# Two fused adaLN/FFN layers on one core: gates by block transposes on VectorE, T1's sums on VectorE, other places for W5's copies and C12's results

## The chip, the cores and the metric

One core of one Trainium2 chip runs the whole program. The metric is the time of one execution in microseconds (us), median of several runs. TensorE (PE in the profile) multiplies, VectorE (DVE), ScalarE (ACT) and GpSimd (POOL) do the elementwise work, SyncE (SP) issues most DMAs.

## The reference, cut to what matters

```python
def layer(x):                              # twice: layer 0, layer 1; x is 8 x 256 tokens of 1024
    c = x @ W0.T + b0 + lora(x, adapter of the batch)            # "cond", rank 16
    probs = softmax(c @ W_router.T)                              # 8 experts
    top2 of probs, renormalized -> w_dense[token, expert], 0 for the other six
    h = einsum('td,erd->ter', c, lora_A)                         # 8 experts x rank 16 = 128 rows
    f = c @ W1.T + b1 + 2.0 * einsum('ter,eor,te->to', h, lora_B, w_dense)
    return x + f
```

## The kernel before

`fused_layers` first multiplies the two dense weights of a layer (the fold: `fold`, lines 489 to 491, E = [W1, lora_A, router], 1160 columns, against W0), then runs the folded product over 2048 tokens. Numbers are fp32, kept as a high and a low part in fp32r; a product of two such numbers takes three matmuls (hi*hi, hi*lo, lo*hi). Whatever is split has its cast on ScalarE (high part) and a subtraction on VectorE (low part, helper `sub`, L977).

Tokens come in chunks of 512; two chunks are a **pair** g (0 and 1 in layer 0, 2 and 3 in layer 1), and a pair's product is done by Strassen-Winograd: seven products W1, W2, W6, W5, W3, W7, W4 of half size, each of four output tiles m of 12 matmuls (L605), on the input blocks B11, B21 (chunk 0), B12, B22 (chunk 1) and the sums T3 = B22 - B12, T2 = T3 + B11, T1 = B22 - T2, T4 = B21 - T2. GpSimd makes the four sums. The results C11, C12, C21, C22 gather in PSUM banks; `keep_w1`, `keep_w5` (ScalarE) and `keep_u2`, `keep_w57` (VectorE) carry partial results out of banks, `out_c11` to `out_c22` (VectorE, L1186) add bias and residual. `low_and_experts` (L621 and three matmuls) adds the adapter and expert parts to a bank.

Each engine runs a fixed list in the order of the code, and semaphores join the lists. For each chunk tb of a pair:

- `routers` (16 matmuls L564, then 24 into H_BANK) yields the low-rank, router and expert rows; `adapters` and `low_rest` on VectorE make `low_mv` of them; `inner_low` (L587) adds the low-rank part to the 128 rows h.
- The logits: four matmuls of 128 x 8 (L609), one to a group of 128 tokens, between the matmuls of a W product. Tokens are then on partitions.
- `routing` (VectorE): bias, `max`, `max_index`, comparison with an iota, softmax of two (`gap`, the exponential on ScalarE in `top_exp`), and `gates`: tokens on partitions, 128 columns.
- Four fp32 transposes on TensorE (L614) turn the gates into H_BANK, in front of which h was copied out by ScalarE (`inner`, h_sb). `gated` multiplies both (hg), ScalarE and VectorE split hg (`hg_split`), and `low_and_experts` needs it.

In chunk 1 TensorE's order is: routers, W6 m0, `inner_low`, W6 m1 to m3, W5 m0 and m1, W3 m0 with `low_and_experts`, W3 m1 with `low_and_experts`, W5 m2 and m3, W3 m2, m3, W7, W4. W3 m adds into the bank of W5 m, so it waits for W5 m's copy (w5_done). W5 needs both parts of T1.

SyncE's list holds the loads of the weight tiles: a ring of seven buffers (`load_ring`, n = 0 to 27 for the 28 tiles of a pair; tile n may load once tile n - 7 is used), between them the stores and the loads of the next pair's blocks. In a pair that has a successor in its layer (pairs 0 and 2), the load of B21 (1 MB) stands ahead of ring loads 23, 24, 25 and waits for r21_done, that is for GpSimd's `add_12`, `make_t4` and `add_21`, twelve additions in a row that begin at the first `keep_u2`. Ring load 23 brings the tile of W7 m3.

## Time and profile before

| | us |
|---|---|
| median of 3 runs (lowest, highest) | 686.79 (685.77, 687.58) |
| the profiled execution: its own time | 686.49 |
| its span, first to last instruction | 684.8 |
| busy in the span: PE, DVE, ACT, POOL | 678.8, 423.3, 231.6, 261.6 |
| chain that ended last: PE's share | 97% |

The page's second part shows PE busy at 9 tenths or more in all slices but the first and the last, and a granted TensorE clock of 9 tenths or more in all. In the timelines below a row is a start in us, a time taken, an engine, a line, an operation and its tiles; "xN" means N instructions in a row merged, and a bracket names idle time ahead of it and who ended it.

### The profile page before, as it was taken

What the parts mean: (1) busy time and instruction counts of PE and PEld (TensorE: products, weight loads), DVE (VectorE), ACT (ScalarE), POOL (GpSimd) and SP (SyncE); (2) the same over time, 40 slices, a digit from 0 to 9 for tenths busy, and PEclk for the clock granted to TensorE, in tenths of its full rate; (3) what the DMA queues carried; (4) which work ended last, traced back from release to release, by engine and by line L of the source; (5) the groups of instructions that cost most, each with busy time, mean ns of one, the idle gap of its engine ahead of it and who ended that gap; (6) DMA issues with size and microseconds to landing.
All of it is one profiled execution on the core that took longest, in us unless ns stands there. A gap on an engine that the chain in (4) does not pass through costs nothing.

```text
span 684.8 us, 9215 instructions
## 1 busy us (share of the span) xinstructions
PE 678.8 (99%) x3299; PEld 598.0 (87%) x3299; DVE 423.3 (62%) x719; ACT 231.6 (34%) x429; POOL 261.6 (38%) x217
## 2 busy tenths in 40 slices
PE   8999999999999999999999999999999999999997
PEld 7999999888888888888899999998888888888886
DVE  5664667868855474862673753788698437738423
ACT  6444244645221034220514344266352302422200
POOL 2373023036583150395134433030647625105930
PEclk9999999999999999999999999999999999999999
DMA  8345756993768944547742755689846886535633
GB/s 291 115 156 185 262 196 205 392 386 130 245 194 327 326 123 124 157 145 254 276 176 72 235 167 182 246 279 371 333 127 212 282 342 196 181 116 168 199 106 123
DMA packets 74132, 147.25 MB, mean 215 GB/s; under 512 B 6948, under 2 KB 38308, under 8 KB 73958
## 3 DMA queue, kind: packets, MB, share of 16 engines
q1 hardware_dynamic: 70678, 138.20, 58.7%
q10 hardware_dynamic: 1872, 6.36, 2.9%
q0 software_dynamic: 1536, 2.10, 1.1%
q8 instruction: 26, 0.43, 0.3%
q14 instruction: 20, 0.16, 0.1%
HBM read 98.42 MB, written 47.33 MB: 213 GB/s over the span
## 4 chain that ended last, share of the span: by engine, by line
PE 97%; DMA 1%; SPq 1%; ACT 0%; DVE 0%; issue 0%
PE ps L605 45%; PE ps L489 15%; PE ps L490 15%; PE ps L491 15%; PE ps L564 4%; PE ps L621 2%; DMA e_raw<-in_ext 1%; PE ps L614 1%; SPq L289 0%; PE ps L587 0%; ACT e_hl L715 0%; SPq L266 0%; DVE w_hl L977 0%; DVE w L1186 0%; ACT w_hl L724 0%
## 5 line engine op out<-in xcount | busy, mean ns | idle before, releaser
L605 PE MATMUL ps<-x_hl,a_hl 128*128 128x512 f32 x1344 | 317.8, 394 | 0.0
L605 PEld LDWEIGHTS ps<-x_hl,a_hl 128*128 128x128 f32 x1344 | 251.3, 188 | 53.3 <-issue 0.3
L489 PE MATMUL ps<-e_hl,w_hl 128*128 128x384 f32 (+1 forms) x432 | 146.2, 338 | 0.8 <-DVE e_hl L977 0.7
L490 PE MATMUL ps<-e_hl,w_hl 128*128 128x384 f32 (+1 forms) x432 | 145.8, 337 | 0.0
L491 PE MATMUL ps<-e_hl,w_hl 128*128 128x384 f32 (+1 forms) x432 | 145.5, 337 | 0.0
L489 PEld LDWEIGHTS ps<-e_hl,w_hl 128*128 128x128 f32 x432 | 81.3, 188 | 2.7 <-issue 1.3
L490 PEld LDWEIGHTS ps<-e_hl,w_hl 128*128 128x128 f32 x432 | 81.3, 188 | 0.0
L491 PEld LDWEIGHTS ps<-e_hl,w_hl 128*128 128x128 f32 x432 | 81.3, 188 | 0.0
L977 DVE TENSOR_TENSOR x_hl<-x_raw,x_hl 128x512 fp32r<-128x512 f32 x64 | 60.8, 1004 | 8.4 <-ACT x_hl L811 8.4
L1363 POOL TENSOR_TENSOR w<-x_raw 128x512 f32<-128x512 f32 x16 | 23.8, 1515 | 103.8 <-DMA x_raw<-in_xT 32.7
L977 DVE TENSOR_TENSOR w_hl<-w_raw,w_hl 128x1024 fp32r<-128x1024 f32 (+2 forms) x24 | 20.6, 868 | 58.0 <-ACT w_hl L702 51.1
L1345 POOL TENSOR_TENSOR f_sum<-p_raw 128x512 f32<-128x512 f32 x8 | 12.5, 1558 | 111.7 <-ACT p_raw L760 111.7
L1382 POOL TENSOR_TENSOR x_sum<-x_raw,c 128x512 f32<-128x512 f32 x16 | 24.2, 1542 | 69.3 <-PE ps L491 69.3
L977 DVE TENSOR_TENSOR x_hl<-x_sum,x_hl 128x512 fp32r<-128x512 f32 x32 | 39.6, 1251 | 15.3 <-ACT x_hl L835 9.8
L1038 DVE SCALAR_TENSOR_TENSOR acc<-e_hl,b_sb,acc 128x1160 f32<-128x1160 f32 x32 | 45.6, 1424 | 0.8
L760 ACT COPY p_raw<-ps 128x384 f32<-128x384 f32 (+1 forms) x48 | 22.3, 480 | 70.0 <-PE ps L491 69.9
L811 ACT CAST x_hl<-x_raw 128x512 fp32r<-128x512 f32 x64 | 35.7, 618 | 26.2 <-PE ps L605 12.9
L1186 DVE SCALAR_TENSOR_TENSOR x_raw<-ps,bias_sb,x_raw 128x512 f32<-128x512 f32 x32 | 22.8, 741 | 32.5 <-PE ps L491 32.3
L1416 POOL TENSOR_TENSOR w<-w,x_raw 128x512 f32<-128x512 f32 x16 | 22.0, 1375 | 36.8 <-DVE w L980 36.8
L1394 POOL TENSOR_TENSOR x_raw<-x_raw,u 128x512 f32<-128x512 f32 x16 | 22.0, 1404 | 29.9 <-DVE u L980 29.9
L564 PE MATMUL ps<-x_hl,s_hl 128*128 128x512 f32 x128 | 31.3, 395 | 0.0
L977 DVE TENSOR_TENSOR px_hl<-p_raw,px_hl 128x128 fp32r<-128x128 f32 x16 | 11.5, 717 | 30.7 <-ACT pr_hl L764 30.7
(118 smaller groups left out, 896.9 us busy)
## 6 DMA issues: line engine op xcount, KB each, us to landing
a_hl<-form_scratch SPq DMA_DIRECT2D x112, 512.0 KB, 5.0
form_scratch<-f_hl SPq DMA_DIRECT2D x56, 512.0 KB, 7.3
...
```

Of the source, the lines that this page charges most:

```text
L489: nc.tensor.matmul(dst, w_hi, m_hi, start=start, stop=False, skip_group_check=again)
L490: nc.tensor.matmul(dst, w_hi, m_lo, start=False, stop=False, skip_group_check=again)
L491: return nc.tensor.matmul(dst, w_lo, m_hi, start=False, stop=stop, skip_group_check=again)
L564: last = nc.tensor.matmul(ps[:, S_BANK, :], s_hl[:, k, :], x_hl[:, slots[block], k % KH, hl, :], start=(k + hl == 0), stop=(k + hl == KT))
L605: last = nc.tensor.matmul(ps[:, bank, :], a_hl[:, n % NM, k, w, :], x_hl[:, slot, k, x, :], start=start and i == 0, stop=i == 3 * KH - 1, ...
L760: ins = nc.scalar.copy(p_raw[:, pair % 2, half, o:o + n], ps[:, fold_bank(r, ob), 0:n])
L811: nc.scalar.copy(x_hl[:, slot, k, 0, :], raw_of(block, k)).then_inc(x_hi[block], 1)
L977: return nc.vector.tensor_tensor(dst, a, b, ALU.subtract)
L1038: ins = nc.vector.scalar_tensor_tensor(acc[:], e_hl[:, k, hl, 0:EXT].bitcast(f32), b0_sb[:, k:k + 1], acc[:], op0=ALU.mult, op1=ALU.add)
L1186: return nc.vector.scalar_tensor_tensor(dst, ps[:, bank, :], bias_sb[:, k:k + 1], rest_of_sum, op0=ALU.add, op1=ALU.add)
L1363: nc.gpsimd.tensor_tensor(w57[:, k, :], raw_of(B22, k), raw_of(B12, k), ALU.subtract).then_inc(S["t3_done"], 1)
L1382: nc.gpsimd.tensor_tensor(x_sum[:, SLOT_OF[g % SUPER][T1], k, 1, :], raw_of(B22, k), c21[:, k, :], ALU.subtract).then_inc(S["t1_done"], 1)
```

## The change

- **Logits.** One matmul of 128 x 512 in `inner_low` takes the place of the four 128 x 8. Its weights `rt_cols` are the eight router columns, copied sixteen times side by side by ScalarE (`router_cols`, one copy of 128x128 for each chunk). Each expert's logit of each token is so on 16 partitions, tokens along the columns.
- **Gates.** `routing` turns the logits by VectorE's transpose of 32 x 32 blocks, so that 16 groups of 32 tokens stand on the partitions; it finds the best two experts by reductions and comparisons (the first of equals by a rank), makes for each 32 partitions the gates of two experts, 16 columns each, and turns them back by blocks into hg. The four transposes on TensorE, the identity matrix and `inner`'s copy are gone. `gated` now multiplies H_BANK with hg, and its low half is a function of its own, `gated_low`.
- **T1.** VectorE makes T1's four sums (`make_t1`, after `low_rest` of chunk 1), not GpSimd. T1's and T3's splits both stand ahead of `routing(g, 1)`.
- **Order.** In chunk 1 TensorE does W3 m0 and W3 m1 one after the other, and then both `low_and_experts`. ScalarE copies W5's m1, m2, m3 ahead of T4's casts. VectorE does `gated`, u2's m0, `gated_low`, u2's other three, then C12's m0 and m1 ahead of T4's splits.

```diff
                 else:
                     pe.wait_ge(S["stack_in"], l + 1)
                 pe.wait_ge(S["eye_done"], 2)
+                pe.wait_ge(S["rt_done"], u + 1)
+                nc.tensor.matmul(ps[:, S_BANK, :], rt_cols[:], low_mv[tb][:], start=True,
+                                 stop=True).then_inc(S["pe_logit"], 1)
                 nc.tensor.matmul(ps[:, H_BANK, :], stack[tb][:, D:D + ER], low_mv[tb][:], start=False,
                                  stop=True).then_inc(S["pe_h"], 1)
 
-            def product(g, j, m, bank, start, logits_of=None, gates_of=None):
+            def product(g, j, m, bank, start):
 
 
...
-
-                    pe.wait_ge(S["h_done"], 2 * g + gates_of + 1)
-                    pe.wait_ge(S["gate_done"], 2 * g + gates_of + 1)
                 for i in range(3 * KH):
                     k, (w, x) = i // 3, ((0, 0), (0, 1), (1, 0))[i % 3]
                     last = nc.tensor.matmul(ps[:, bank, :], a_hl[:, n % NM, k, w, :], x_hl[:, slot, k, x, :],
                                             start=start and i == 0, stop=i == 3 * KH - 1, skip_group_check=not start)
-                    if logits_of is not None and i < TT:
-                        tb = logits_of
-                        logit = nc.tensor.matmul(ps[:, S_BANK, i * NE:(i + 1) * NE], low_mv[tb][:, i * P:(i + 1) * P],
-                                                 stack[tb][:, D + ER:EXT], start=True, stop=True)
-                        if i == TT - 1:
-                            logit.then_inc(S["pe_logit"], 1)
-                    if gates_of is not None and i < TT:
-                        gate = nc.tensor.transpose(ps[:, H_BANK, i * P:(i + 1) * P], gates[:, i, :], ident_sb[:])
-                        if i == TT - 1:
-                            gate.then_inc(S["pe_gate"], 1)
                 last.then_inc(S["pe_m"], 1)
 
             def low_and_experts(half, tb, m, bank, start=False):
...
                                 pe.wait_ge(S["u2_done"], KH * g + m - 1)
-                            product(g, W5, m, BANK_C12[m], True, gates_of=None if m else 1)
+                            product(g, W5, m, BANK_C12[m], True)
                         for m in (m2, m2 + 1):
                             pe.wait_ge(S["w5_done"], KH * g + m + 1)
                             product(g, W3, m, BANK_C12[m], False)
-                            if m == 0:
-                                pe.wait_ge(S["hg_lo"], 2 * g + 2)
-                            low_and_experts(0, 1, m, BANK_C12[m])
+                            if m >= 2:
+                                low_and_experts(0, 1, m, BANK_C12[m])
+                        if m2 == 0:
+                            pe.wait_ge(S["hg_lo"], 2 * g + 2)
+                            for m in range(2):
+                                low_and_experts(0, 1, m, BANK_C12[m])
...
 
+            def router_cols(l, g, tb):
+
...
+                               stack[tb][:, D + ER:EXT].bitcast(f32).unsqueeze(1).broadcast_to([P, P // NE, NE])
+                               ).then_inc(S["rt_done"], 1)
+
             def first_stack(l):
...
                     adapters(l, g, 1, more)
-                    t1_split(g, range(2))
-                    inner(g, 1)
-                    t1_split(g, range(2, 3))
+                    router_cols(l, g, 1)
+                    t1_split(g)
                     top_exp(g, 1)
-                    t1_split(g, range(3, 4))
                     keep_w5(g, 0)
                     hg_split(g, 1)
-                    keep_w5(g, 1)
+                    for m in range(1, KH):
+                        keep_w5(g, m)
                     t4_split(g)
-                    for m in range(2, KH):
-                        keep_w5(g, m)
...
+            def make_t1(g):
+
+                dve.wait_ge(S["pe_hx"], 2 * g + 2)
+                for k in range(KH):
+                    dve.wait_ge(S["t2_done"], KH * g + k + 1)
+                    sub(x_sum[:, SLOT_OF[g % SUPER][T1], k, 1, :], raw_of(B22, k), c21[:, k, :]
+                        ).then_inc(S["t1_done"], 1)
+
...
+                ins = nc.vector.transpose(by_token[:].rearrange("p g c -> p (g c)"), ps[:, S_BANK, :])
+                ins.then_inc(S["logit_read"], 1)
+                dve.wait_ge(S["logit_read"], u + 1)
+                chain(nc.vector.tensor_tensor(lg, lg,
+                                              bias_r[:].unsqueeze(1).broadcast_to([P, GR, NE]), ALU.add))
+                for i, (v, m, gate) in enumerate(((lg, ma, ga), (lg2, mb, gb))):
+                    chain(nc.vector.tensor_reduce(top[i][:], v, AXIS.X, ALU.max))
+                    chain(nc.vector.tensor_tensor(m[:], v, over(top[i], NE), ALU.is_equal))
+                    if i:
+                        sub(gap[:], top[1][:], top[0][:]).then_inc(S["gap_done"], 1)
+                    chain(nc.vector.tensor_tensor(m[:], m[:], ranks, ALU.mult))
+                    chain(nc.vector.tensor_reduce(first_of[i][:], m[:], AXIS.X, ALU.max))
+                    if i == 0:
+                        chain(nc.vector.tensor_tensor(m[:], over(first_of[i], NE), ranks, ALU.is_equal))
+                        chain(nc.vector.scalar_tensor_tensor(lg2, m[:], -3.0e38, lg, op0=ALU.mult, op1=ALU.add), False)
+                    chain(nc.vector.tensor_tensor(gate[:], over(first_of[i], WANT), wanted, ALU.is_equal))
                 dve.wait_ge(S["exp_done"], u + 1)
                 chain(nc.vector.tensor_scalar(den[:], ex[:], 1.0, None, ALU.add))
                 chain(nc.vector.reciprocal(wb[:], den[:]))
                 chain(nc.vector.tensor_scalar(wa[:], wb[:], 2.0, None, ALU.mult))
-                chain(nc.vector.tensor_tensor(den[:], ex[:], wa[:], ALU.mult))
-                chain(nc.vector.tensor_tensor(ma[:], ma[:], wa[:].broadcast_to([P, TT, NE]), ALU.mult), False)
-                chain(nc.vector.tensor_tensor(mb[:], mb[:], den[:].broadcast_to([P, TT, NE]), ALU.mult))
-                nc.vector.tensor_tensor(gates[:].rearrange("p t (e r) -> p (t e) r", r=R),
-                                        *(m[:].rearrange("p t e -> p (t e)").unsqueeze(2)
-                                          .broadcast_to([P, TT * NE, R]) for m in (ma, mb)),
-                                        ALU.add).then_inc(S["gate_done"], 1)
+                chain(nc.vector.tensor_tensor(den[:], ex[:], wa[:], ALU.mult), False)
+                chain(nc.vector.tensor_tensor(ga[:], ga[:], over(wa, WANT), ALU.mult))
+                chain(nc.vector.tensor_tensor(gb[:], gb[:], over(den, WANT), ALU.mult))
+                chain(nc.vector.tensor_tensor(by_token[:].rearrange("p g (n r) -> p g n r", r=R),
+                                              *(m[:].unsqueeze(3).broadcast_to([P, GR, WANT, R]) for m in (ga, gb)),
+                                              ALU.add))
+                chain(nc.vector.transpose(hg[:], by_token[:].rearrange("p g c -> p (g c)")))
 
             def gated(g, tb):
                 u = 2 * g + tb
-                dve.wait_ge(S["h_done"], u + 1)
-                dve.wait_ge(S["pe_gate"], u + 1)
-                nc.vector.scalar_tensor_tensor(hg[:], h_sb[:], bias_sb[:, KT:KT + 1], ps[:, H_BANK, :],
+                dve.wait_ge(S["pe_h"], u + 1)
+                nc.vector.scalar_tensor_tensor(hg[:], ps[:, H_BANK, :], bias_sb[:, KT:KT + 1], hg[:],
                                                op0=ALU.add, op1=ALU.mult).then_inc(S["hg_done"], 1)
-                dve.wait_ge(S["hg_hi"], u + 1)
+
+            def gated_low(g, tb):
+                dve.wait_ge(S["hg_hi"], 2 * g + tb + 1)
                 sub(hg_hl[:, tb, 1, :], hg[:], hg_hl[:, tb, 0, :].bitcast(f32)).then_inc(S["hg_lo"], 1)
 
...
                     low_rest(g, 1)
+                    make_t1(g)
                     out_c11(g, 2)
                     out_c11(g, 3)
-                    made_split(g, T1, range(2))
+                    made_split(g, T1)
+                    sum_split(g, T3, w57)
                     routing(g, 1)
-                    made_split(g, T1, range(2, 4))
-                    sum_split(g, T3, w57)
-                    for m in range(KH):
+                    gated(g, 1)
+                    keep_u2(g, 0)
+                    gated_low(g, 1)
+                    for m in range(1, KH):
                         keep_u2(g, m)
-                    gated(g, 1)
                     if more:
                         s_split(l, 2 * s + 2)
+                    out_c12(g, 0)
+                    out_c12(g, 1)
                     made_split(g, T4)
-                    for m in range(KH):
-                        out_c12(g, m)
+                    out_c12(g, 2)
+                    out_c12(g, 3)
                     if more:
...
                 for s in range(SUPER):
                     g = SUPER * l + s
-                    for k in range(KH):
-                        make_t1(g, k)
                     for m in range(KH):
                         add_12(g, m)
                     for k in range(KH):
```

TensorE, pair 0, chunk 1, from the last tile ahead of `inner_low` (low_mv_86 and stack_68 are chunk 1's buffers), before:

```order
L605 MATMUL ps<-x_hl,a_hl 128x512 x12
L587 MATMUL ps<-low_mv_86,stack_68 128x512
L605 MATMUL ps<-x_hl,a_hl 128x512
L609 MATMUL ps<-stack_68,low_mv_86 128x8
L605 MATMUL ps<-x_hl,a_hl 128x512
L609 MATMUL ps<-stack_68,low_mv_86 128x8
L605 MATMUL ps<-x_hl,a_hl 128x512
L609 MATMUL ps<-stack_68,low_mv_86 128x8
L605 MATMUL ps<-x_hl,a_hl 128x512
L609 MATMUL ps<-stack_68,low_mv_86 128x8
```

and after:

```order
L607 MATMUL ps<-x_hl,a_hl 128x512 x12
L591 MATMUL ps<-low_mv_86,rt_cols 128x512
L593 MATMUL ps<-low_mv_86,stack_68 128x512
L607 MATMUL ps<-x_hl,a_hl 128x512 x84
L613 MATMUL ps<-low_mv_86,stack_68 128x512
```

The eight small matmuls are gone from between the W matmuls, one of full width has come in front of the one that was there, and 84 W matmuls now stand together.

VectorE, pair 0, chunk 1, from C11's first two results to the start of `routing`, before:

```order
L1186 SCALAR_TENSOR_TENSOR x_raw<-ps,bias_sb,x_raw 128x512 x2
L1138 SCALAR_TENSOR_TENSOR low_mv_86<-sx_r,sign_sb,ps 32x512
L977 TENSOR_TENSOR low_mv_86<-sx,low_mv_86 32x512
L1186 SCALAR_TENSOR_TENSOR x_raw<-ps,bias_sb,x_raw 128x512 x2
L977 TENSOR_TENSOR x_hl<-x_sum,x_hl 128x512 x2
L1148 TENSOR_TENSOR lg<-ps,bias_r 128x32
```

and after:

```order
L1207 SCALAR_TENSOR_TENSOR x_raw<-ps,bias_sb,x_raw 128x512 x2
L1151 SCALAR_TENSOR_TENSOR low_mv_86<-sx_r,sign_sb,ps 32x512
L982 TENSOR_TENSOR low_mv_86<-sx,low_mv_86 32x512
L982 TENSOR_TENSOR x_sum<-x_raw,c_62 128x512 x4
L1207 SCALAR_TENSOR_TENSOR x_raw<-ps,bias_sb,x_raw 128x512 x2
L982 TENSOR_TENSOR x_hl<-x_sum,x_hl 128x512 x4
L982 TENSOR_TENSOR x_hl<-w_61,x_hl 128x512 x4
L1167 STREAM_TRANSPOSE by_token<-ps 128x512
```

T1's sums (x_sum) came in, and T1's last two and T3's four splits (x_hl from x_sum and from w_61) moved from behind `routing` to ahead of it.

ScalarE, pair 0, chunk 1, from T1's casts to T4's casts (w_61 is W5's copy, hg_hl the high part of hg), before:

```order
L817 CAST x_hl<-x_sum 128x512 x2
L867 COPY h_sb<-ps 128x512
L817 CAST x_hl<-x_sum 128x512
L871 ACTIVATE ex<-gap 128x4
L817 CAST x_hl<-x_sum 128x512
L893 COPY w_61<-ps 128x512
L877 CAST hg_hl<-hg 128x512
L893 COPY w_61<-ps 128x512
L835 CAST x_hl<-x_sum 128x512 x4
L893 COPY w_61<-ps 128x512 x2
```

and after:

```order
L860 CAST rt_cols<-stack_68 128x128
L811 CAST x_hl<-x_sum 128x512 x4
L879 ACTIVATE ex<-gap 128x16
L901 COPY w_61<-ps 128x512
L885 CAST hg_hl<-hg 128x512
L901 COPY w_61<-ps 128x512 x3
L829 CAST x_hl<-x_sum 128x512 x4
```

`inner`'s copy h_sb went, the router columns' copy came, and W5's m2 and m3 moved ahead of T4's four casts (x_sum). W5's m1 stands behind the cast of hg as before.

## Rows read from the trace of the kernel before

**Rows 1.** The page's first part: busy us (share of span) and instructions.
```profile
PE 678.8 (99%) x3299; PEld 598.0 (87%) x3299; DVE 423.3 (62%) x719; ACT 231.6 (34%) x429; POOL 261.6 (38%) x217
```

**Rows 2.** Waits of TensorE: who waited for whom, us, times, longest.
```profile
PE ps L489 <- DVE e_hl L977: 0.7, 2, 0.4
```

**Rows 3.** Groups of instructions, TensorE: busy us, mean ns, idle before.
```profile
L614 PE MATMUL ps<-ident_sb,gates 128*128 128x128 f32 x32 | 8.7, 272 | 0.0
L609 PE MATMUL ps<-stack,low_mv 128*128 128x8 f32 x32 | 5.4, 168 | 0.0
```

**Rows 4.** TensorE's timeline, chunk 1 of pair 0: start us, us taken, instruction.
```profile
166.60 2.88 PE L605 MATMUL ps<-x_hl,a_hl 128*128 128x512 f32 x12
...
169.54 0.39 PE L605 MATMUL ps<-x_hl,a_hl 128*128 128x512 f32 x1
...
186.84 0.39 PE L621 MATMUL ps<-low_mv,stack 128*128 128x512 f32 x1
...
204.07 21.92 PE L605 MATMUL ps<-x_hl,a_hl 128*128 128x512 f32 x96
```

**Rows 5.** VectorE's timeline in the same stretch.
```profile
162.91 0.87 DVE L1122 TENSOR_SCALAR low_b<-ps,mul_sb 32x256 f32<-32x256 f32 x2
...
166.03 0.76 DVE L1138 SCALAR_TENSOR_TENSOR low_mv<-sx_r,sign_sb,ps 32x512 fp32r<-32x512 f32 x1
...
167.54 1.41 DVE L1186 SCALAR_TENSOR_TENSOR x_raw<-ps,bias_sb,x_raw 128x512 f32<-128x512 f32 x2
...
177.30 2.49 DVE L977 TENSOR_TENSOR x_hl<-w,x_hl 128x512 fp32r<-128x512 f32 x4
179.70 2.48 DVE L980 TENSOR_TENSOR u<-ps,u 128x512 f32<-128x512 f32 x4
182.10 0.74 DVE L1179 SCALAR_TENSOR_TENSOR hg<-h_sb,bias_sb,ps 128x512 f32<-128x512 f32 x1
```

**Rows 6.** Groups, VectorE, whole run: operations like the new ones.
```profile
L1102 DVE STREAM_TRANSPOSE acc_t<-acc 128x1152 f32<-128x1152 f32 x2 | 2.7, 1356 | 0.0
...
L1107 DVE TENSOR_REDUCE part_sb<-acc_t 128x36 f32<-128x1152 f32 x2 | 2.7, 1345 | 0.0
...
L1159 DVE TENSOR_TENSOR ma<-iota_sb,top_f 128x32 f32<-128x32 f32 x8 | 1.5, 193 | 0.3
```

**Rows 7.** ScalarE's timeline, same stretch.
```profile
182.87 0.62 ACT L877 CAST hg_hl<-hg 128x512 fp32r<-128x512 f32 x1 [0.69 <-DVE hg L1179]
```

**Rows 8.** GpSimd's timeline, same stretch.
```profile
166.91 6.40 POOL L1382 TENSOR_TENSOR x_sum<-x_raw,c 128x512 f32<-128x512 f32 x4 [5.40 <-PE ps L491]
180.47 5.49 POOL L1394 TENSOR_TENSOR x_raw<-x_raw,u 128x512 f32<-128x512 f32 x4 [7.16 <-DVE u L980]
...
192.00 5.95 POOL L1403 TENSOR_TENSOR c<-x_raw,u 128x512 f32<-128x512 f32 x4
```

**Rows 9.** SyncE's queue, same stretch: start of issue, us.
```profile
197.98 0.38 SPq L360 DMA_DIRECT2D x_raw<-in_xT  x1
198.46 1.84 SPq L373 DMA_DIRECT2D a_hl<-form_scratch  x3
```

**Rows 10.** Ring load 23 of pair 0, issued at 198.46.
```profile
DMA to landing us min/median/max: 8.5/8.5/8.5
```

**Rows 11.** The same load of pair 2, issued at 535.71.
```profile
DMA to landing us min/median/max: 9.1/9.1/9.1
```

**Rows 12.** GpSimd's timeline, chunk 1 of pair 1: T1's sums.
```profile
278.09 4.23 POOL L1382 TENSOR_TENSOR x_sum<-x_raw,c 128x512 f32<-128x512 f32 x3 [29.12 <-PE ps L491]
```

**Rows 13.** TensorE's timeline there: W6 begins.
```profile
277.78 2.88 PE L605 MATMUL ps<-x_hl,a_hl 128*128 128x512 f32 x12
```

**Rows 14.** TensorE's timeline, chunk 0 of pair 0.
```profile
136.41 0.39 PE L587 MATMUL ps<-low_mv,stack 128*128 128x512 f32 x1
```

**Rows 15.** ScalarE's timeline, chunk 0 of pair 0.
```profile
136.84 0.58 ACT L867 COPY h_sb<-ps 128x512 f32<-128x512 f32 x1 [1.64 <-PE ps L587]
...
139.08 1.07 ACT L888 COPY u<-ps 128x512 f32<-128x512 f32 x2
```

109 lines of the change are left out of this document (54 added, 55 removed).

## The prediction

> **What bounds the kernel now.** The first view to read is the page's busy line: TensorE is busy 678.8 of 684.8 us [rows 1]. That alone could hide pauses, since the ends of matmuls are modelled, so the second view is the list of TensorE's waits: behind the start-up only 0.7 us in two pieces, both in the fold, and none in the token stage [rows 2]. Every matmul there starts as soon as the one ahead lets it, so the kernel is a queue of TensorE work, and two questions decide the change: what the removed and added matmuls cost in that queue, and whether any wait that was early before is now late. Durations don't answer the first. The groups give 272 ns for a transpose and 168 ns for a logit matmul [rows 3], but neighbours overlap. The timeline does: 96 W matmuls in a row take 21.92 us; less the last one's own 0.39 that is 21.53 us between 96 starts, 0.2266 us each. Between 169.54 and 186.84 there are 72 of them (W6 m1 to m3, W5 m0 and m1, W3 m0), four logit matmuls and four transposes [rows 4]. 72 x 0.2266 = 16.32 of the 17.30 us; so eight small ones cost 0.98 us, 0.12 each.
>
> **TensorE's sum.** There are eight chunks. Removed: 8 x 0.98 = 7.8 us. Added: eight matmuls of 128 x 512, 8 x 0.2266 = 1.8 us. Net 6.0 us less, all of it on the path. The low bound is that a chunk's eight cost no more than 0.9 (some of the 0.98 could be the hand-over at `inner_low`): 5.4 less. A higher bound than 6.0 has no row. The Trainium skill (TensorE: Matmul & The Clock Gate, Part 4: PE-mode transpose) gives about 275 ns for a transpose in a kernel's context; the duration in this trace agrees, 272. Taken as cost in the queue it would make the 32 transposes alone worth 8.8 us, against 32 x 0.12 = 3.9 by the timeline, and the time would come out about 5 us lower than below. I take the timeline.
>
> **New lateness, chunk 1 of pair 0.** Both chunks' savings move TensorE ahead: 0.75 us (0.98 - 0.23) by the start of chunk 1's W6, 1.50 by its W3. VectorE doesn't move with it, since its chain starts at 162.91 behind T2's splits, which hang on loads and GpSimd [rows 5]. So I walk that chain. Up to 167.54 nothing changes. Then T1's sums: four subtractions of 128x512 at the spacing of T3's splits, which ran with GpSimd idle (177.30 to 179.70, 0.60 each), 2.40, to 169.94. C11's pair 1.42, to 171.36. T1's four splits 2.40, T3's 2.40, to 176.16. GpSimd has nothing until u2, so none of these is slowed.
>
> The new `routing` isn't in the trace; its price comes from like operations [rows 6]. A line through 193 ns for 32 elements and 1356 ns for 1152 has 1.04 ns per element; a reduction of 1152 costs the same (1345). That makes 0.69 us for 512 elements, 0.29 for 128, 0.19 for 32 and 0.17 for 16. Nearly every one waits for the one ahead, which I put at 0.04 (VectorE's hg ends at 182.84 and ScalarE starts on it at 182.87 [rows 5, 7]). Two transposes and the last addition, 3 x 0.73 = 2.2; eleven of 128 elements, 11 x 0.33 = 3.6; four of 32, 0.9; five of 16, 1.0; less 0.2 where there is no wait: 7.5 us. Between 6.8 (all handovers free) and 9 (0.06 more on each of 24) is possible.
>
> So `gated` starts at 183.66 and hg is ready at 184.40 (0.74 [rows 5]). **W5's m1** is copied by ScalarE only behind hg's cast: 184.43 + 0.62 [rows 7] + 0.54 = 185.6. W3 m1 wants it at 186.84 + 0.91 (the four matmuls of `low_and_experts`), less 0.91 since these now stand behind W3 m1 as well, less 1.50: 185.34. **0.3 us late**, in a place where nothing was late before. hg's low half itself is ready by 186.4 at the latest, wanted at 188.1.
>
> **Ring load 23.** `keep_u2` m0 comes behind `gated`: 183.66 + 0.66 + 0.69 = 185.0, where it used to release GpSimd by 180.47. GpSimd's twelve additions took 180.47 to 197.95 [rows 8], 17.5 us; with fewer of VectorE's two-input operations beside them perhaps 16.5. r21_done comes at 201.5 to 202.5. The 1 MB load of B21 left at 197.98, with r21_done, and ring load 23 0.48 us behind it [rows 9], landing 8.5 us later [rows 10]. It now lands at 210.5 to 211.5. W7 m3 wants it at 204.07 + 3 x 2.72 - 1.50 = 210.73 [rows 4]. The wait was covered by 5 us before and is now at its edge: pair 0 loses 0.3 to 0.8 in all (the two delays are one behind the other, not added). Pair 2 is built alike, but there the same load takes 9.1 us [rows 11]: 0.4 to 1.5. Pairs 1 and 3 have no such load. There, T1's sums can start 0.31 us behind W6's first matmul (GpSimd did, at 278.09 against 277.78 [rows 12, 13]), in pair 0 1.69 behind (167.54 against 166.60 - 0.75), so their chain has 1.4 us more and W5's copy comes 1.1 early. Both pairs together: 0.7 to 2.3 us lost, I take 1.5, in the middle, since the unknowns lie on both sides.
>
> **Chunk 0.** In pairs 0 and 2 ScalarE's exponential stands ahead of `keep_w1` m0, which W2 m0 wants. The matmul's result is seen 0.43 us after its start (136.41 to 136.84 [rows 14, 15]); gap is ready 4.0 us into routing by the same prices; exponential and copy 0.14 + 0.6 [rows 15]: 5.2 after `inner_low` starts. W2 m0 comes after two matmuls and two tiles, 26 x 0.2266 = 5.9. Covered by 0.7. In pairs 1 and 3 m0 is copied earlier and three tiles lie between. **At nothing** stand: GpSimd's four T1 sums (6.4 us [rows 8], GpSimd isn't waited for there), the copy of the router columns (some 0.3 us of ScalarE, 1.5 us ahead of need behind the adapters' copies), `inner`'s copy, C12's new place (its stores leave earlier), the smaller constants.
>
> **The sum.** 684.8 - 6.0 + 1.5 = 680.3 of span; the execution's own time is 1.7 above its span, 682.0, and the median 0.3 above that execution (686.79 against 686.49): **682.3 us**.
>
> **Rivals.**
> 1. Nothing comes late: routing at 6.8 or GpSimd's twelve at under 16.5. 686.8 - 6.0 = 680.8. For it: both delays are tenths on chains of 20 to 40 us. Against: two places would have to be covered in two pairs.
> 2. The reload takes the gain: stores, B21 and rings 23 to 27 are now issued closer together, and ring 23 lands 10 to 11 us after issue. Pairs 0 and 2 then lose some 2.5 each: 686.8 - 6.0 + 5.0 = 685.8. For it: 9.1 us in pair 2 already. Against: ring load 22 and C12's first stores are out of the way by then.
> 3. Slower: `routing` on VectorE sets the end. If it takes x us more than 7.5, pairs 0 and 2 lose x each in chunk 1, and beyond 1.1 the other pairs', beyond 0.7 chunk 0 of pairs 0 and 2: 2x + 2(x - 1.1) + 2(x - 0.7). That and the 1.5 above eat the 6.0 at x = 1.35, a routing of 8.9 us; at x = 2, 691. Place: ScalarE's `hg_split` and `top_exp`, with W5's and W1's copies queued behind. Against: the lines above fit three kinds of operation. The Trainium skill (VectorE: DVE Perf Modes, Rules for kernel authors) sends 128x128 transposes to TensorE where PSUM will do, and asks for few operations in a chain on VectorE; both speak for this rival. No row here shows a chain of 128-element operations.
> 4. The matmul of 128 x 512 doesn't take the normal slot, or the small ones were free: the sum is 2 to 3 less, about 685. Rows 4 speak against it.
>
> **Chances.** Forecast 0.55; rival 1 0.17; rival 2 0.14; rival 3 0.08; rival 4 0.06. The range of 8 in 10 goes from rival 1 to near rival 2: 680.7 to 685.5. A measurement tells about 0.3%, 2.1 us, from no change. Faster by more (below 684.7): 0.55 + 0.17 + parts of 2 and 4, 0.80. Within: 0.13. Slower: 0.07.
>
> **What would show it.** In the changed kernel's trace: TensorE with 56 matmuls fewer (64 gone, 8 come), W matmuls still 0.2266 apart; `routing` from transpose to `gated` 7.5 us; a pause of TensorE ahead of W3 m1 on ScalarE's copy w and one ahead of W7 m3 on a DMA of a_hl, in pairs 0 and 2 only; T1's sums at 0.6 us each. Wrong would be: pauses in chunk 0, routing above 8.5 us, or any pause in pairs 1 and 3.

## The result, and the profile after

| | before | changed |
|---|---|---|
| median, us | 686.50 (685.77 to 687.58, 6 runs) | 681.44 (680.25 to 681.99, 6 runs) |
| profiled execution, us | 686.49 | 681.37 |
| its span, us | 684.8 | 679.7 |

The ratio is 0.9922, 95% interval 0.9912 to 0.9933: the changed kernel is 5.1 us, 0.8%, faster. The forecast was 682.3 (680.7 to 685.5).

The page's first part, to be read beside [rows 1] (busy us, share of the span, instructions):

```profile
PE 673.0 (99%) x3243; PEld 592.9 (87%) x3243; DVE 467.6 (69%) x724; ACT 226.6 (33%) x429; POOL 238.7 (35%) x201
```

TensorE has 56 instructions less and 5.8 us less of busy time. VectorE has 44 us more, 69% instead of 62%, and that in itself cost nothing. What it did cost stands in TensorE's waits (who waited for whom, us in all, times, longest), beside [rows 2]:

```profile
PE ps L621 <- DVE hg_hl L1239: 1.6, 1, 1.6
PE ps L607 <- ACT w L901: 0.6, 2, 0.4
PE ps L492 <- DVE e_hl L982: 0.6, 2, 0.4
PE ps L607 <- DMA a_hl<-form_scratch: 0.2, 1, 0.2
```

The first is the start-up and the third the fold, both as before. The second and the fourth are new: the token stage, which had no pause, has three. In TensorE's timeline (start, us taken, instruction, idle before it and who ended that) they are:

```profile
150.42 2.97 PE L607 MATMUL ps<-x_hl,a_hl 128*128 128x512 f32 x12 [0.21 <-DMA a_hl<-form_scratch]
...
169.77 15.80 PE L607 MATMUL ps<-x_hl,a_hl 128*128 128x512 f32 x69
185.98 3.04 PE L607 MATMUL ps<-x_hl,a_hl 128*128 128x512 f32 x12 [0.41 <-ACT w L901]
...
203.36 11.95 PE L607 MATMUL ps<-x_hl,a_hl 128*128 128x512 f32 x52
...
519.79 3.02 PE L607 MATMUL ps<-x_hl,a_hl 128*128 128x512 f32 x12 [0.20 <-ACT w L901]
```

The first line is W2 m3 in chunk 0 of pair 0, the lines at 185.98 and 519.79 are W3 m1 in chunk 1 of pairs 0 and 2. A pause costs 0.16 us more than the idle time in brackets, since a matmul's 0.39 is counted to its end while the next may start 0.2266 after its start. So the three cost 0.37, 0.57 and 0.36: 1.3 us. The matmuls right behind a pause are a little slower too (3.04 us for twelve instead of 2.88), 0.4 us in all. No row after 203.36 shows a wait for ring load 23. Pairs 1 and 3 have no pause at all.

VectorE's timeline, chunk 1 of pair 0, is the chain that the prediction walked; lines between the first and the second transpose are routing's small operations:

```profile
167.93 2.50 DVE L982 TENSOR_TENSOR x_sum<-x_raw,c 128x512 f32<-128x512 f32 x4
170.46 1.41 DVE L1207 SCALAR_TENSOR_TENSOR x_raw<-ps,bias_sb,x_raw 128x512 f32<-128x512 f32 x2
171.79 2.49 DVE L982 TENSOR_TENSOR x_hl<-x_sum,x_hl 128x512 fp32r<-128x512 f32 x4
174.19 2.49 DVE L982 TENSOR_TENSOR x_hl<-w,x_hl 128x512 fp32r<-128x512 f32 x4
176.59 0.71 DVE L1167 STREAM_TRANSPOSE by_token<-ps 128x512 f32<-128x512 f32 x1
...
183.29 0.71 DVE L1193 STREAM_TRANSPOSE hg<-by_token 128x512 f32<-128x512 f32 x1
184.04 0.75 DVE L1198 SCALAR_TENSOR_TENSOR hg<-ps,bias_sb,hg 128x512 f32<-128x512 f32 x1
...
185.48 1.81 DVE L982 TENSOR_TENSOR hg_hl<-hg,hg_hl 128x512 fp32r<-128x512 f32 x1
```

Routing takes 184.04 - 176.59 = 7.45 us. ScalarE's timeline there shows W5 m1's copy behind hg's cast:

```profile
184.82 0.62 ACT L885 CAST hg_hl<-hg 128x512 fp32r<-128x512 f32 x1 [3.42 <-DVE hg L1198]
185.35 0.58 ACT L901 COPY w<-ps 128x512 f32<-128x512 f32 x1
```

The chain that ended last was TensorE's for 97% of the span before and is for 75% now. From the pause ahead of W3 m1 it goes back through this copy and VectorE's chain to GpSimd's T2, and from there to the 1 MB load of B22 (start, us until it landed):

```profile
134.85 14.19 DMA x_raw<-in_xT
```

So the pause on ScalarE's copy also begins with a DMA. This load let GpSimd start at 149.16, where it started at 148.78 before, and VectorE's chain began 0.4 us later with it (163.31 for 162.91).

### The profile page after: what moved, and what is told of

Same layout as the page of the kernel before. It is cut to its first block, busy times and chain, and to the rows that moved or that the text cites. A ratio compares the mean times of both kernels' runs of the same rounds, so it can differ in the third digit from the quotient of the medians.

```text
span 679.7 us, 9094 instructions
## 1 busy us (share of the span) xinstructions
PE 673.0 (99%) x3243; PEld 592.9 (87%) x3243; DVE 467.6 (69%) x724; ACT 226.6 (33%) x429; POOL 238.7 (35%) x201
## 4 chain that ended last, share of the span: by engine, by line
PE 75%; DMA 9%; DVE 8%; POOL 3%; SPq 2%; issue 2%; ACT 1%; POOLq 0%; ACTq 0%
PE ps L607 33%; PE ps L492 13%; PE ps L493 12%; PE ps L494 12%; DMA form_scratch<-f_hl 4%; PE ps L567 2%; DMA x_raw<-in_xT 2%; DMA x_raw<-x_scratch 2%; PE ps L613 2%; POOL w L1393 2%; DVE x_hl L982 2%; POOL c L1405 1%; DVE f_hl L982 1%; DMA e_raw<-in_ext 1%; DVE x_raw L1207 1%
## 5 line engine op out<-in xcount | busy, mean ns | idle before, releaser
L607 PE MATMUL ps<-x_hl,a_hl 128*128 128x512 f32 x1344 | 310.1, 390 | 0.8 <-ACT w L901 0.6
L982 DVE TENSOR_TENSOR x_hl<-x_raw,x_hl 128x512 fp32r<-128x512 f32 x64 | 70.5, 1154 | 3.9 <-ACT x_hl L805 3.8
L1393 POOL TENSOR_TENSOR w<-x_raw 128x512 f32<-128x512 f32 x16 | 25.6, 1633 | 107.3 <-DMA x_raw<-in_xT 33.3
L1375 POOL TENSOR_TENSOR f_sum<-p_raw 128x512 f32<-128x512 f32 x8 | 12.5, 1566 | 111.3 <-ACT p_raw L755 111.3
L982 DVE TENSOR_TENSOR x_hl<-x_sum,x_hl 128x512 fp32r<-128x512 f32 x32 | 35.5, 1169 | 23.3 <-ACT x_hl L829 23.3
L1207 DVE SCALAR_TENSOR_TENSOR c<-ps,bias_sb,c 128x512 f32<-128x512 f32 x16 | 11.7, 749 | 26.2 <-PE ps L494 26.2
L567 PEld LDWEIGHTS ps<-x_hl,s_hl 128*128 128x128 f32 x128 | 23.8, 188 | 5.6 <-DVE x_hl L982 0.9
```

The lines of the kernel that those rows point to most:

```text
L567: last = nc.tensor.matmul(ps[:, S_BANK, :], s_hl[:, k, :], x_hl[:, slots[block], k % KH, hl, :], start=(k + hl == 0), stop=(k + hl == KT))
L607: last = nc.tensor.matmul(ps[:, bank, :], a_hl[:, n % NM, k, w, :], x_hl[:, slot, k, x, :], start=start and i == 0, stop=i == 3 * KH - 1, ...
L982: return nc.vector.tensor_tensor(dst, a, b, ALU.subtract)
L1393: nc.gpsimd.tensor_tensor(w57[:, k, :], raw_of(B22, k), raw_of(B12, k), ALU.subtract).then_inc(S["t3_done"], 1)
```

## The experiments

A plain median stands beside the span of the one profiled execution, and a ratio is always to executions of the kernel before that were timed together with that run (medians 686.23 to 686.51). Expectations were written before each run.

### Parts of the change alone

**w5_ahead**: is the pause ahead of W3 m1 the place of W5 m1's copy behind hg's cast?

```diff
                     keep_w5(g, 0)
+                    keep_w5(g, 1)
                     hg_split(g, 1)
-                    for m in range(1, KH):
+                    for m in range(2, KH):
                         keep_w5(g, m)
```

> The changed kernel with one edit: in chunk 1 ScalarE copies W5's m1 ahead of hg's cast instead of behind it. Theory (TensorE's queue less 6.0 us, and what is missing to that is two late copies): the two pauses ahead of W3 m1 (W3 m1 started 0.57 us late in pair 0 and 0.37 in pair 2 by the changed kernel's trace) are gone, span 679.7 - 0.9 = 678.8, time about 680.5. Rival (these pauses are paid somewhere else anyway, by hg's cast, which now comes later, or by ring load 23): the span stays at 679.5 to 679.9 and a new pause of the same size stands ahead of low_and_experts or of W7 m3.

Measured: 681.01 (679.55 to 682.25), ratio 0.9923 (0.9909 to 0.9936), span 680.5. Both pauses on the copy are gone, as said, and still the span of the profiled execution, the slowest of five, is no shorter, because the other kind has grown. TensorE's waits, and its timeline in chunk 0 of pair 0:

```profile
PE ps L607 <- DMA a_hl<-form_scratch: 1.2, 2, 0.8
PE ps L492 <- DVE e_hl L983: 1.2, 1, 1.2
...
148.42 2.99 PE L607 MATMUL ps<-x_hl,a_hl 128*128 128x512 f32 x12 [0.47 <-DMA a_hl<-form_scratch]
152.16 3.00 PE L607 MATMUL ps<-x_hl,a_hl 128*128 128x512 f32 x12 [0.75 <-DMA a_hl<-form_scratch]
```

W2 m2 and W2 m3 wait there for ring loads 6 and 7 (1.5 us with the 0.16 of each), and the fold lost 0.6 more than in the changed kernel's execution. Over all executions the ratio is the changed kernel's, 0.9923 against 0.9922. So the 0.9 us of the edit are seen in the waits, not in the times; and there is a second cause, of which the prediction knew nothing, that varies from one execution to the next.

**t1_alone**: the kernel before, with T1's sums on VectorE only.

```diff
+                    make_t1(g)
                     out_c11(g, 2)
...
-                    for k in range(KH):
-                        make_t1(g, k)
                     for m in range(KH):
                         add_12(g, m)
```

> The kernel before with one part of the change: VectorE makes T1's four sums, GpSimd does not; nothing else. Theory (the gain is TensorE's queue alone): nothing late, TensorE has the same matmuls, 686.5 within 0.5 us. Rival (part of the gain comes from the port that VectorE and GpSimd share, or from the order of the elementwise work): 1 to 3 us faster, 683.5 to 685.5. T1's sums should take 0.6 us each on VectorE, T1's last split be ready near 177.8 us of pair 0, wanted at 178.2.

Measured: 685.93 (685.83 to 686.66), ratio 0.9999 (0.9989 to 1.0008), span 684.2. GpSimd is relieved and nobody waited for it: nothing gained.

**t1_gpsimd**: the changed kernel with T1's sums back on GpSimd (the same edit, turned round).

> The changed kernel with T1's sums back on GpSimd, all else as changed. GpSimd's four take some 5.6 to 6.4 us from W6's first matmul on, so T1's last split ends near 174.2 us of pair 0 and routing starts near 176.6, the same as with VectorE's sums. Theory: the move of T1 is worth between nothing and 0.6 us in a pair, the time is 681.4 to 683. Rival (the move is what keeps the longer chain on VectorE in time): pauses of 1 to 2 us in each pair ahead of W3 m1, 685 to 689.

Measured: 680.73 (680.62 to 682.52), ratio 0.9922 (0.9907 to 0.9937), span 680.8. No difference can be measured. In the trace VectorE reaches routing at 176.02 instead of 176.59, the copy comes 0.6 earlier, and the pause ahead of W3 m1 is gone. That isn't the edit's doing: VectorE's chain began 0.67 earlier in this execution (162.64 for 163.31), and from there to routing it took 13.4 us against 13.3. VectorE is rid of 2.5 us of sums, but what runs beside GpSimd's sums is slower, T1's splits (4.50 us instead of 2.49) and `low_rest`'s subtraction (1.29 instead of 0.68):

```profile
162.64 0.87 DVE L1135 TENSOR_SCALAR low_b<-ps,mul_sb 32x256 f32<-32x256 f32 x2
...
166.00 5.94 POOL L1411 TENSOR_TENSOR x_sum<-x_raw,c 128x512 f32<-128x512 f32 x4 [4.77 <-PE ps L494]
...
166.55 1.29 DVE L982 TENSOR_TENSOR low_mv<-sx,low_mv 32x512 fp32r<-32x512 f32 x1
...
169.19 4.50 DVE L982 TENSOR_TENSOR x_hl<-x_sum,x_hl 128x512 fp32r<-128x512 f32 x4
```

So the place of T1's sums is worth nothing, as was expected. This execution, the slowest of four, lost 1.6 us on ring loads 6 and 7 again, in pair 2.

**w3_order_before**: the changed kernel with TensorE's old order, `low_and_experts` m0 between W3 m0 and W3 m1.

```diff
+                            if m == 0:
+                                pe.wait_ge(S["hg_lo"], 2 * g + 2)
+                            low_and_experts(0, 1, m, BANK_C12[m])
-                            if m >= 2:
-                                low_and_experts(0, 1, m, BANK_C12[m])
-                        if m2 == 0:
-                            pe.wait_ge(S["hg_lo"], 2 * g + 2)
-                            for m in range(2):
-                                low_and_experts(0, 1, m, BANK_C12[m])
```

> The changed kernel with TensorE's old order in chunk 1: W3 m0, its low_and_experts, W3 m1, its low_and_experts. The low half of hg is then wanted 2.7 us earlier, at 185.4 in pair 0, and was ready at 187.3 in the changed kernel. Theory: a wait on hg_hl of 1.9 us in pairs 0 and 2 takes the place of the 0.57 and 0.37, and 0.1 in pairs 1 and 3; together some 2.9 more, 684.3 us. Rival (the low half's 1.81 us are an effect of GpSimd beside it and the order hides nothing that counts): 681.4 to 682.5.

Measured: 684.39 (684.21 to 685.14), ratio 0.9974 (0.9965 to 0.9984), span 683.2. As expected: hg's low half is late by 1.5 and 1.7 us in pairs 0 and 2.

```profile
186.94 0.50 PE L613 MATMUL ps<-low_mv,stack 128*128 128x512 f32 x1 [1.53 <-DVE hg_hl L979]
```

**c12_behind_t4** and **w5_behind_t4**: the two moves of VectorE's and ScalarE's order, undone one at a time.

```diff
-                    out_c12(g, 0)
-                    out_c12(g, 1)
                     made_split(g, T4)
-                    out_c12(g, 2)
-                    out_c12(g, 3)
+                    for m in range(KH):
+                        out_c12(g, m)
```

> Edit: the changed kernel, with C12's first two results again behind T4's splits on VectorE (the kernel before had all four there); their stores leave SP's queue ahead of ring loads 22 and 23. In the changed kernel T4's splits end at 203.8 in pair 0, so C12 m0's store would leave at about 204.7 and ring load 22 right behind it at 205 (191.2 now); it lands 4.5 to 5.8 later, 209.5 to 210.7, and W7 m2 wants it at 208.8. Ring load 23, behind a store and B21's 1 MB, lands at 213 to 214, wanted 211.5 plus what is already lost. Expected 2 lost in each of pairs 0 and 2, 1 in each of pairs 1 and 3: +6, 687.4 (684 to 690), pauses on a_hl ahead of W7 m2 and m3. Rival (C12's place was worth nothing, as the prediction has it under the edits at nothing): 681.4 to 682.

Measured: 691.29 (688.66 to 692.36), ratio 1.0067 (1.0045 to 1.0088), span 688.8: more than expected. The pauses are where they were said to be (TensorE, pair 0):

```profile
209.44 3.00 PE L607 MATMUL ps<-x_hl,a_hl 128*128 128x512 f32 x12 [0.75 <-DMA a_hl<-form_scratch]
214.50 13.87 PE L607 MATMUL ps<-x_hl,a_hl 128*128 128x512 f32 x60 [2.06 <-DMA a_hl<-form_scratch]
```

and each pair pays 0.9 (pair 3) to 3.1, 8.5 in all.

```diff
                     keep_w5(g, 0)
                     hg_split(g, 1)
-                    for m in range(1, KH):
-                        keep_w5(g, m)
+                    keep_w5(g, 1)
                     t4_split(g)
+                    for m in range(2, KH):
+                        keep_w5(g, m)
```

> Edit: the changed kernel, with ScalarE's copies of W5 m2 and m3 behind T4's casts, where the kernel before had them. T4's sums end at 196.9 in pair 0, the last cast at 197.5, W5 m2's copy then at 198.0; W3 m2 wants it at 196.1. Expected 1.9 lost in pairs 0 and 2 (of which what is lost here gives ring load 23 time, nothing back), 0.7 in pairs 1 and 3: +5.1, 686.5 (685 to 689), pauses on ScalarE's copy w ahead of W3 m2. Rival (that place was worth nothing): 681.4 to 682.

Measured: 692.56 (692.35 to 695.35), ratio 1.0099 (1.0075 to 1.0122), span 690.9: double of what was expected. TensorE waits in all four pairs, ahead of W3 m2, 2.8 in pairs 0 and 2 and 1.5 in pairs 1 and 3. T4's last sum ended at 197.57, 0.7 later than taken: its splits on VectorE now ran beside the sums, which took 5.91 us for 5.03. And in pair 0 the pause itself has a price. The timeline and the windows of 3 us (busy us of each engine and instructions, then the granted clock, DMA share, GB/s):

```profile
198.75 4.62 PE L607 MATMUL ps<-x_hl,a_hl 128*128 128x512 f32 x12 [2.78 <-ACT w L901]
...
198.00:201.00 3.00, 2.25 (x7) 1.81 (x8) 1.66 (x2) 1.19 (x3) 3.00 (x3) 0.77 0.00 0
201.00:204.00 3.00, 3.00 (x10) 2.33 (x10) 0.00 (x0) 0.00 (x0) 3.00 (x3) 0.66 0.00 0
```

Twelve matmuls take 4.62 us where they take 2.88: part of them ran at the lower of the clock's two levels, 1.2 GHz, after TensorE had stood still for 2.8 us. That is 1.7 us on top of the pause. So both moves are needed: each, left out, costs about twice what the whole change brings. In the kernel before, which had no pause there, they weren't, since T4's splits were over at 194.3 there; in the changed one GpSimd is done with T4's sums only at 196.9.

### What the small ones cost in the queue

Four matmuls of 128x8 (more_small), or four transposes of 128x128 (more_turns), put back in each chunk at places where nothing waits for them: one behind each of the first four matmuls of W2 m1 and of W5 m2.

```diff
                                             start=start and i == 0, stop=i == 3 * KH - 1, skip_group_check=not start)
+                    if more_of is not None and i < TT:
...
+                        nc.tensor.transpose(ps[:, S_BANK, i * P:(i + 1) * P], ident_sb[:], ident_sb[:])
```

> Edit: the changed kernel, and in each chunk TensorE does four more matmuls of 128x8 (the old logit matmuls again, their result unused), one behind each of the first four matmuls of W2 m1 (chunk 0) and of W5 m2 (chunk 1). Nothing waits for them. By the timeline of the kernel before, a main matmul with a small one behind it takes 0.34 instead of 0.2266 us, so 32 x 0.115 = 3.7 us; the four of chunk 0 stand ahead of W3 m1 of the same pair and give W5 m1's copy and the ring loads time, which takes back up to 0.9. Expected 681.4 + 3.7 - 0.9 = 684.2, TensorE's pauses on ScalarE's copy w gone or under 0.2. Rival (a small one costs its duration, 168 ns): 32 x 0.168 - 0.9 = +4.5, 685.9. Rival (it is free in the queue): 680.5 to 681.4.

> Edit: the changed kernel, and at the same places as in more_small four fp32 transposes of 128x128 (the old gate transposes' form, of the identity, their result unused). By the timeline of the kernel before, 0.34 instead of 0.2266 us with one behind it: 32 x 0.115 = 3.7, less the 0.9 that it covers: 684.2, the same as for the small ones. Rival (a transpose costs its duration of 272 ns, as the Trainium skill's page TensorE: Matmul & The Clock Gate gives it with 275 in context): 32 x 0.272 - 0.9 = +7.8, 689.2.

Measured: more_small 685.09 (684.28 to 686.72), span 682.6; more_turns 685.49 (684.45 to 686.69), span 683.0. The two agree to 0.4 us. Were the duration the price, the transposes would cost 32 x (0.272 - 0.168) = 3.3 us more than the small matmuls. The Trainium skill's 275 ns for a transpose (TensorE: Matmul & The Clock Gate, Part 4) is met by its duration here, 0.27 in the row below, and not by what it takes from the queue. TensorE's timeline of more_turns shows the same 0.34 from main matmul to main matmul as before the change:

```profile
145.81 0.27 PE L614 MATMUL ps<-ident_sb 128*128 128x128 f32 x1
145.84 0.48 PE L608 MATMUL ps<-x_hl,a_hl 128*128 128x512 f32 x1
...
146.18 0.48 PE L608 MATMUL ps<-x_hl,a_hl 128*128 128x512 f32 x1
```

By spans they cost 2.9 and 3.3 over the changed kernel, against 2.8 expected, and no pause is left in the token stage of either. The medians are higher, at +3.7 and +4.1 (+4.3 and +4.5 by ratios). more_small alone would fit its duration rival (+4.5) as well; it is the transposes, which by theirs would have cost 7.8, that decide. The profiled execution of more_small is the fastest of its ten, so its span is a low one. The price in the queue can be read without the pauses: in pair 1, which has none, TensorE takes 93.16 us from the first W matmul to the last in the changed kernel (241.44 to 334.60), 94.09 with the eight small matmuls and 94.15 with the eight transposes, so 0.12 us for each of either kind. That is 3.7 and 4.0 us for 32. The medians rose by about that much, so little of the 0.9 us that was to be taken back shows in them; why, these runs don't tell.

### The ring loads at the end of chunk 0

Where do the pauses on ring loads come from? Their place is the end of chunk 0 in pairs 0 and 2, behind a fold. The windows of 36 us there, of the kernel before and then of the changed one, agree in the DMA share (the last number but one), 1.04: the DMA engines are busy without a gap.

```profile
118.00:154.00 36.00, 36.00 (x167) 29.75 (x166) 28.07 (x70) 19.66 (x35) 5.22 (x4) 1.00 1.04 384
```
```profile
118.00:154.00 36.00, 35.79 (x161) 29.46 (x160) 30.89 (x67) 18.99 (x35) 4.84 (x4) 1.00 1.04 384
```

Ring load 7 was issued at 137.43 before, and at 135.34 in the changed kernel; the time to landing, in the same order:

```profile
DMA to landing us min/median/max: 12.5/12.5/12.5
```
```profile
DMA to landing us min/median/max: 14.9/14.9/14.9
```

It landed at 149.9 before and lands at 150.2 now: asking 2 us earlier changed nothing in a queue as full as this. W2 m3 wanted it at 151.2 before (twelve matmuls ahead of 153.90, where `low_and_experts` began) and wants it at 150.05 now. The cover of 1.25 us is used up: TensorE wants the load 1.13 earlier (0.75 by the change, 0.4 because the fold ahead happened to end earlier in this execution), and it lands 0.3 later. Two runs put that to the test, with one more copy of 512 KB in the queue, behind B22's load and ahead of ring load 7, in the changed kernel (extra_load) and in the kernel before (extra_load_before):

```diff
                 load_x(l, 0, B22)
+                sp.dma_start(spare[l], xT[0:P, 0:2 * CH]).then_inc(S["d_spare"], 16)
```

> Edit: the changed kernel, and SP's queue has one more copy of 512 KB, from the input to a spare place in DRAM, between the load of B22 and ring load 7 in the first pair of each layer (pairs 0 and 2). Nothing waits for it. Question: the changed kernel's one pause in chunk 0, 0.2 us ahead of W2 m3 on ring load 7, where DMA engines are busy from 118 to 154. Theory: what TensorE gained there has used up the cover of the ring loads (1.5 us before), so 512 KB at the 415 GB/s of that stretch, 1.26 us, come out nearly whole in pairs 0 and 2: pauses on a_hl of 1 to 1.5 us in each, 681.4 + 2.3 = 683.7. If a copy from DRAM to DRAM takes twice its bytes: up to 686. Rival (the 0.2 is scatter of one execution and there is still cover): 681.4 to 682.

> Edit: the kernel before, with the same extra copy of 512 KB at the same place. Theory: ring load 7 landed there 1.5 us ahead of W2 m3, so 1.26 us more are covered: 686.3 to 686.8, no pause on a_hl over 0.3. If the copy takes twice its bytes (2.5 us): +1 in pairs 0 and 2, 688.5. Rival (the cover was the same in both kernels): the same increment as extra_load shows over the changed kernel.

Measured: extra_load 684.56 (682.16 to 688.81), ratio 0.9981 (0.9959 to 1.0003), span 683.1; extra_load_before 687.65 (686.44 to 690.22), ratio 1.0017 (1.0004 to 1.0030), span 687.2. TensorE's waits of the two:

```profile
PE ps L609 <- DMA a_hl<-form_scratch: 4.3, 3, 2.0
```
```profile
PE ps L607 <- DMA a_hl<-form_scratch: 2.5, 2, 1.6
```

By medians the copy costs 3.1 us in the changed kernel and 1.4 in the one before (by ratios 4.0 and 1.2). In pair 0 of the kernel before W2 m3 waited 0.95 + 0.16, with 1.25 of cover gone first, so ring load 7 came 2.4 us later: near to twice the 1.26 us that its bytes alone would take, the second of the two cases in the expectation. But the delay isn't the same everywhere. By issue and landing, ring load 7 came 2.2 and 3.7 us later in pairs 0 and 2 of the kernel before, 1.2 and 4.2 in those of the changed one, so what such a copy costs the queue stays open. In either case the kernel before pays what is beyond its cover, and the changed one most of it: the pauses, with the 0.16 of each, are 2.9 us against 4.7. With the copy in both, the change is worth 0.36% (about 0.26 either way) instead of 0.78%, so some half of its gain is lost to it. The rival of an equal increment is the less likely, though the intervals are wide (extra_load's runs lie 6.6 us apart, the changed kernel's 1.7).

**ring6_first** is the version that follows: w5_ahead, and ring load 6 ahead of the stack's loads and of the 580 KB store.

```diff
                 load_ring(l, 0, 5)
+                load_ring(l, 0, 6)
                 first_stack(l)
                 sp.dma_start(bw_dram[l], bw_st[2 * LOW:P, :, :].bitcast(f32)).then_inc(S["d_bw"], 16)
-                load_ring(l, 0, 6)
```

> Edit: the changed kernel, with ScalarE's copy of W5 m1 ahead of hg's cast (as in w5_ahead, which took the two pauses on it away) and ring load 6 ahead of the stack's loads and the 580 KB store of bw_scratch in SP's queue. Theory: what is left of pauses in the token stage is ring loads 6 and 7 at the end of chunk 0, 0 to 1.3 us by execution; load 6 is then on time, load 7 still at its edge. Span 678.3 to 679.0, median 680.3 (679.8 to 680.9), a few tenths below w5_ahead and at the limit of what these runs tell. Rival (ring load 7 is late by the same bytes anyway): as w5_ahead, 681.0.

Measured: 680.32 (680.10 to 680.84), ratio 0.9910 (0.9894 to 0.9927), span 678.4. TensorE's waits have only start-up and fold left:

```profile
PE ps L621 <- DVE hg_hl L1240: 1.6, 1, 1.6
PE ps L492 <- DVE e_hl L983: 0.4, 1, 0.4
PE ps L567 <- DVE x_hl L983: 0.2, 1, 0.2
```

It is the lowest median of all, and what was expected of it; against the changed kernel's 0.9922 (0.9912 to 0.9933) the intervals overlap, so the 1.1 us are seen in the waits rather than proved by the times.

### How much a longer routing costs

**routing_plus2**: four memsets of hg inside routing. They add x = 2.64 us, not 2.1 (each 0.48, and 0.17 waiting for the one ahead).

```diff
                 dve.wait_ge(S["logit_read"], u + 1)
+                for _ in range(4):
+                    chain(nc.vector.memset(hg[:], 0.0))
```

> Edit: the changed kernel, and VectorE writes zeros to hg four times (128x512, some 0.5 us each, 2.1 in all; a row of the run gives the exact x) inside routing, behind the first transpose, in every chunk. It sizes how far routing's length decides. Theory, from the changed kernel's rows: in chunk 1 of pairs 0 and 2 W5 m1's copy is already late, so x comes out whole (2 x 2.1); in pairs 1 and 3 it has 1.25 us of cover (2 x 0.85). In chunk 0 of pairs 0 and 2 there is a stall of about 1.4 (cover 0.7), but it isn't added: chunk 1's chain on VectorE hangs on loads, so TensorE's lateness in chunk 0 is time that chunk 1's wait then has. Sum +5.9: 687.3. Rival (the formula of rival 3 in the prediction, which adds chunk 0's stalls): 4.2 + 2.0 + 2.8 = 9.0 less nothing, 690.4. Rival (the pauses are scatter, and routing has cover): under +3, 684.

Measured: 693.15 (692.81 to 693.86), ratio 1.0093 (1.0076 to 1.0110), span 692.2: 12.5 over the changed kernel's. TensorE's waits and its timeline in pair 0:

```profile
PE ps L607 <- ACT w L901: 5.1, 4, 1.4
PE ps L607 <- ACT u L896: 3.7, 2, 1.9
...
144.80 12.79 PE L607 MATMUL ps<-x_hl,a_hl 128*128 128x512 f32 x48 [1.86 <-ACT u L896]
```

The formula of rival 3, with chunk 0's stalls added, gives 2 x 2.64 + 2 x 1.54 + 2 x 1.94 = 12.2. The theory that chunk 1 absorbs them, with the right x, gives 5.3 + 2.8 = 8.1. By the total the formula hits and the theory misses, but the pauses say otherwise. All six together cost 9.8 us, where the changed kernel lost 0.9 on the copy: 8.9 more, near to the theory (6.1 in pairs 0 and 2 for its 5.3, 2.8 in pairs 1 and 3 as it says). VectorE's timeline says why: T1's sums now wait for TensorE.

```profile
170.32 2.50 DVE L982 TENSOR_TENSOR x_sum<-x_raw,c 128x512 f32<-128x512 f32 x4 [0.85 <-PE ps L494]
```

Once chunk 0 has delayed TensorE, the chain of pairs 0 and 2 hangs on TensorE as in pairs 1 and 3 and has their cover, and W3 m1 is late by 1.4 to 1.6 in every pair. The stall in chunk 0 is 1.86 + 0.16 = 2.0, against 2.64 - 0.7 = 1.9 by the prediction's cover. So the formula's terms for chunk 0 and for pairs 1 and 3 hold (1.9 and 1.5 forecast, 2.0 and 1.4 measured), and its term for chunk 1 of pairs 0 and 2 fails: it has them pay 2.64 more each, and they pay 0.8 and 1.2 more. Its total is right by luck. The rest of the 12.5 us is no wait in the token stage: 48 matmuls took 12.79 us instead of 11.04 behind the first pause, with a granted clock of 0.64 in 145 to 148 and 0.79 in 148 to 151, matmuls behind the other pauses were some 0.8 slower in all, and the folds and the start took 1.3 more in this execution; against that, the 0.4 on a ring load is gone. The like pause of pair 2 had no such drop of the clock (485.62, 11.19 us).

## Why the prediction was right, step by step

- **TensorE's sum: right.** 56 instructions fewer. 69 matmuls of the changed kernel take 15.80 us, 0.2266 from start to start. From a layer's first W matmul to its last TensorE took 205.81 and 206.01 us before and takes 204.04 and 203.37 now, 4.4 less; with the 1.7 us of pauses and slower matmuls behind them the queue lost 6.1. The other 0.7 of the span is scatter of the folds and the start (the token stage of pair 0 began at 130.56 for 130.97). Two executions without any pause in that stage give it directly: 202.87 us in each layer in ring6_first (130.49 to 333.36), 205.81 in t1_alone (130.71 to 336.52), 5.9 us for both layers. more_small and more_turns confirm that the timeline's 0.12 was the price and the duration wasn't.
- **The walk along VectorE: right.** T1's sums 0.6 each; routing was to begin at 176.16 and began at 176.59, was to take 7.5 and took 7.45; W5 m1's copy was to be late by 0.3 and was late by 0.57 in pair 0 and 0.36 in pair 2. What pair 0 has more is the chain's start, 0.4 later behind B22's load, which the walk took as fixed. One reading of it was wrong without harm: hg's low half was to be ready by 186.4 and was at 187.29, since its subtraction took 1.81 us beside GpSimd, where it takes 0.69 alone; it was wanted at 188.86. w3_order_before shows what it costs where it is wanted earlier. By groups, the transposes of 512 elements took 0.71 us and operations of 128 elements 0.29, as the line through [rows 6] had it.
- **Pairs 1 and 3, chunk 0's chain: right.** No pause in pairs 1 and 3 (cover 1.25, forecast 1.1). In chunk 0 of pair 0 ScalarE's copy for W2 m0 began at 140.64, 0.54 long, for a use at 141.89: covered by 0.7, as said.
- **Ring load 23: wrong in size, both ways.** GpSimd's twelve additions ended at 203.27, later than the 201.5 to 202.5 of the forecast: they ran from 185.47, 0.5 later than forecast, and took 17.8 us, not 16.5. The additions themselves took 16.6, as forecast; the other 1.2 is GpSimd's wait for u2 m1, which now stands behind `gated_low`, and which the forecast left out. But the load landed 5.8 us after issue in both pairs, where [rows 10] and [rows 11] had 8.5 and 9.1. The issue and the landing:

```profile
203.30 0.38 SPq L363 DMA_DIRECT2D x_raw<-in_xT  x1
203.78 1.62 SPq L376 DMA_DIRECT2D a_hl<-form_scratch  x3
...
DMA to landing us min/median/max: 5.8/5.8/5.8
```

  The 3 us ahead of the issue, before and after, say why (next to last number: DMA share):

```profile
195.00:198.00 3.00, 3.00 (x15) 2.49 (x14) 0.61 (x1) 0.59 (x1) 3.00 (x4) 1.00 0.74 164
```
```profile
201.00:204.00 3.00, 3.00 (x15) 2.50 (x14) 3.00 (x3) 1.34 (x3) 3.00 (x3) 1.00 0.00 0
```

  Time to landing isn't a property of a load: before, it shared the DMA engines with earlier ones; now they stood idle. It landed at 209.6, 1.9 us ahead of its use at 211.5. Of the 1.5 us of lateness this term was 0.9 (the copies were the other 2 x 0.3), and it is nothing.
- **Chunk 0's ring loads: missed.** The prediction said that a pause in chunk 0 would be wrong, and there is one, 0.37 us, on a cause it never looked at. The step that failed is the walk itself: TensorE was moved ahead by 0.75 us in chunk 0 ("At nothing" doesn't list them either), and of those who feed it only VectorE and ScalarE were followed, not the ring loads, which can't follow. It costs 0.4 in the profiled execution, 1.5 and 1.6 in those of w5_ahead and t1_gpsimd.
- **At nothing: not what they look like.** C12's new place and the copies of W5 m2 and m3 bring nothing, but 9.8 and 11.1 us would be lost without them, as the runs without them show.
- **The sum**: 680.3 of span forecast, 679.7 measured. Lateness was put at 1.5 and came to 1.3 of pauses, but made of other parts: the copy 0.9 for 0.6, ring load 23 nothing for 0.9, chunk 0's ring load 0.4 for nothing. That these cancel is luck, and so is part of the rest, the folds' scatter.
